# Holding back the second group's weight loads until the fifth x has been turned

## The reference

```
x = x + einsum('bct,bcd->bdt', x, L0_weights[cond])       # 32 x (128 x 128), contracts the 128 channels
x = x + einsum('bsi,boi->bso', x, L1_weight[adapter])     # 32 x (2048 x 2048), contracts the 2048 columns
```

## Time and profile before

| | |
|---|---|
| median of three executions | 1530.03 us |
| the profiled execution's own time | 1530.53 us |
| its span in the profile | 1528.7 us |
| TensorE matmul busy | 1494.1 us (98%) |
| VectorE busy | 1018.4 us (67%) |
| ScalarE busy | 512.9 us (34%) |
| GpSimd busy | 1082.0 us (71%) |
| DMA, mean over the span | 171 GB/s |
| mean granted TensorE clock | 0.992 of full |

### The profile page before, as it was taken

The page is one execution under the profiler, slowest core; times in us unless marked ns, Lnnn a source line. Parts: engine busy times, 40 slices in busy tenths (PEclk is TensorE's granted clock), DMA queues, the critical chain, the costliest instruction groups (busy, mean ns, idle before and its releaser), DMA issues.

```text
span 1528.7 us, 28816 instructions
## 1 busy us (share of the span) xinstructions
PE 1494.1 (98%) x6534; PEld 1231.5 (81%) x6535; DVE 1018.4 (67%) x637; ACT 512.9 (34%) x786; POOL 1082.0 (71%) x659
## 2 busy tenths in 40 slices
PE   5889999999999999999999999999999999999998
PEld 4668888888888888888888888888888888888887
DVE  6582879849592397794957257977768528797521
ACT  2333333333333333333333333333333333333332
POOL 4577778767685687776777578777777667787653
PEclk9979999999999999999999999999999999999999
DMA  7886899989795599897979469989788858998543
GB/s 157 171 188 145 186 188 198 182 179 191 163 206 130 130 202 181 175 202 171 200 160 205 114 153 201 189 181 204 164 186 177 168 119 177 188 204 180 126 110 86
DMA packets 287461, 261.33 MB, mean 171 GB/s; under 512 B 18648, under 2 KB 207064, under 8 KB 287448
## 3 DMA queue, kind: packets, MB, share of 16 engines
q10 hardware_dynamic: 108864, 173.06, 49.5%
q1 hardware_dynamic: 178584, 88.12, 32.6%
HBM read 227.56 MB, written 33.55 MB: 171 GB/s over the span
## 4 chain that ended last, share of the span: by engine, by line
PE 93%; SPq 2%; POOL 1%; DMA 1%; issue 1%; DVE 0%; ACT 0%; ACTq 0%; DVEq 0%
PE z_ps L686 29%; PE z_ps L687 29%; PE z_ps L695 29%; PE out_ps L707 2%; PE out_ps L704 2%; PE out_ps L705 2%; SPq L205 1%; POOL x_low L251 1%; DMA x_nat<-in_x 1%; SPq L196 0%; POOL z_low L257 0%; DMA w_nat<-in_L_cond_weight 0%; DMA ids_row<-in_itok_B 0%; SPq L213 0%; ACT z_high L333 0%
## 5 line engine op out<-in xcount | busy, mean ns | idle before, releaser
L686 PE MATMUL z_ps<-w_high,x_high 128*128 x1984 | 775.9, 391 | 8.1 <-ACT x_high L326 6.5
L687 PE MATMUL z_ps<-w_low,x_high 128*128 x1984 | 775.4, 391 | 0.0
L251 POOL TENSOR_TENSOR x_low<-x_turn,x_high 128x1024 fp32r<-128x1024 f32 x248 | 627.7, 2552 | 16.9 <-ACT x_high L326 16.6
L561 DVE STREAM_TRANSPOSE x_turn<-x_nat 128x1024 f32<-128x1024 f32 x250 | 295.7, 1220 | 454.3 <-DMA x_nat<-in_x 454.1
L695 PE MATMUL z_ps<-w_high,x_low 128*128 x1984 | 469.8, 389 | 0.0
L686 PEld LDWEIGHTS z_ps<-w_high,x_high 128*128 128x128 f32 x1984 | 374.9, 189 | 86.8 <-issue 8.8
L687 PEld LDWEIGHTS z_ps<-w_low,x_high 128*128 128x128 f32 x1984 | 374.8, 189 | 77.9
L695 PEld LDWEIGHTS z_ps<-w_high,x_low 128*128 128x128 f32 x1984 | 372.5, 188 | 77.2
L257 POOL TENSOR_TENSOR z_low<-z_raw,z_high 128x512 fp32r<-128x512 f32 x127 | 167.6, 1320 | 238.7 <-ACT z_high L333 238.7
L341 ACT ACTIVATE out_sb<-out_ps 128x512 f32<-128x512 f32 x128 | 76.5, 597 | 618.6 <-PE out_ps L707 616.6
L326 ACT ACTIVATE x_high<-x_turn 128x1024 fp32r<-128x1024 f32 x248 | 251.5, 1061 | 21.8 <-DVE x_turn L561 20.5
(11 more groups left out here) (92 smaller groups left out, 297.6 us busy)
## 6 DMA issues: line engine op xcount, KB each, us to landing
x_nat<-in_x ACTq DMA_DIRECT2D x500, 256.0 KB, 5.2
w_nat<-in_L_cond_weight SPq DMA_DIRECT2D x320, 256.0 KB, 7.7
out<-out_sb ACTq DMA_DIRECT2D x128, 256.0 KB, 5.7
a_full<-in_L_cond_weights ACTq DMA_DIRECT2D x128, 64.0 KB, 5.5
x_nat<-in_x SPq DMA_DIRECT2D x64, 64.0 KB, 3.0
ids_row<-in_itok_B SPq DMA_DIRECT2D x1, 16.0 KB, 3.0
cond_i<-in_itok_B SPq DMA_DIRECT2D x1, 0.5 KB
expert_i<-in_itok_B SPq DMA_DIRECT2D x1, 0.5 KB
```

What stands on the lines that cost most here:

```text
L251: nc.gpsimd.tensor_tensor(x_low[s][:, half], x_turn[:, half], x_high[s][:, half], ALU.subtract)\
L561: nc.vector.transpose(x_turn[:].rearrange("p (k a c) -> p k a c", a=QUAD, c=SQ)[:, blocks], x_nat[:].rearrange("p (a k c) -> p k a c", a=Q ...
L686: nc.tensor.matmul(z_ps[s][:], xs, w_high[:, ds(at + k * NC, NC)], start=(k == 0), stop=False)
L687: nc.tensor.matmul(z_ps[s][:], xs, w_low[:, ds(at + k * NC, NC)], start=False, stop=False)
```

## The change

One wait is added on SyncE, between the ramp's loads and the loop over the groups. `RAMP` is 4, and VectorE gives `x_turned` a start value of 2 * RAMP = 8, so the value 10 is reached when both halves of the fifth x have been turned.

```diff
             sp.wait_ge(tables_made, 2)
+            sp.wait_ge(x_turned, 2 * RAMP + 2)
             with sp.Fori(1, count_groups(sp)) as q:
                 row = of_group(sp, ROW, q, rows.shape[0] - NC)
                 for m in range(PIECES):
                     load_piece(q, m, row)
```

## The result

| | before | changed |
|---|---|---|
| median, 13 executions each | 1530.56 us | 1533.69 us |
| lowest to highest | 1529.52 to 1531.51 | 1532.14 to 1534.65 |
| the profiled execution's own time | 1530.53 us | 1532.14 us |
| its span | 1528.7 us | 1530.3 us |

The changed kernel is 3.1 us slower: ratio 1.002, 95% interval 1.0011 to 1.0028. The forecast was 1533.5 us, slower. The profiled execution of the changed kernel is the lowest of its thirteen, so the two profiles lie only 1.6 us apart.

What follows compares the result with a forecast made beforehand. The start of step 5 was taken as the bound: the fifth x's -4.6 us does not reach it, the new path through W and the sixth x adds 3.5, giving 1534.0 profiled, 1533.5 us median; range 1529.0 to 1536.0.

Steps and rivals of the forecast that it cites:

- The fifth x: Behind the ramp: lands at 64.4 instead of 69.0, so 4.6 us of TensorE's 6.5 us gap before step 4 go.
- SyncE's issue: After the added wait: 1.6 us of table reads, then first W issue at 68.4, fifteen us later than before.
- W's landing: First piece of W, competing with the sixth x: fourth load lands at 81.2, bounded by 75.3 and 82.5.
- third rival: Clearly slower: W's piece lands behind step 0's output too, step 5 1.3 us later still; chance 0.15.
- The piece's preparation: VectorE's work on W's first piece before turning the sixth x: 6.3 us with handovers, cast at its minimum.
- T to step 5: From T, the start of VectorE's turn of the sixth x (forecast 87.5), through GpSimd's work to step 5: 14.4 us.
- Step 5: TensorE's step 5 starts at 101.9 us instead of 98.44, 3.5 us later.
- The clock: TensorE's half clock around step 5, expected again as before: nothing in the sum, 1 us in the range.
- The time: Whole kernel: 1534.0 us for the profiled execution, 1533.5 us against the median.
- clearly slower: Piece lands behind the output and half clock reaches further into step 5: +1.3 and +1 on +3.5, 1535.6 us; chance 0.15.
- Cover: Behind step 5: W's second group, wanted by step 10, and the seventh x, turned at T + 10.6, cost nothing.
- The faster rival: W's first piece lands by about 76, decided at 76.7; step 5 4.5 us sooner, 1525.5 us; chance 0.10.

Runs made afterwards that it cites:

- the second profile: The changed kernel, unaltered, profiled and timed once more for the spread of the dates; 1533.18 us.
- shorter hold: Against the changed kernel, SyncE waits for the landing of the fifth x instead of its turn; 1528.80 us, ratio 0.999 to the kernel before.
- three x ahead: Against the changed kernel, SyncE held until the sixth x is turned too, VectorE turning sixth and seventh x before W's first piece, later ones each before a piece; 1517.92 us.
- every x ahead: Against the changed kernel, same hold, VectorE turns every x of the start ahead of the piece of W it stood behind; 1523.07 us.
- the longer hold: Against the changed kernel, SyncE waits until the low part of the fifth x is made instead of its turn; 1534.37 us, ratio 1.0023 to the kernel before.

## Why the prediction was right

- *The fifth x* was forecast to land at 64.4 and to let step 4 start at 67.0: turned from 64.11, step 4 at 66.69.
- *SyncE's issue* at 68.4: 68.12. The 1.6 us of table reads behind the wait are real, and ScalarE's first load of the sixth x, at 67.20, does come first.
- *W's landing* at 81.2: 80.5, 0.7 us less, but not for the reason given. The sum rested on loads being served about in their order of issue, with the output of step 0 behind the piece. They were not: the output, issued at 70.37, landed at 77.8, ahead of W's third load (69.16, landed 78.8) and its fourth (80.5), and so it did in the second profile.

```profile
out<-out_sb ACTq DMA_DIRECT2D x1, 256.0 KB, 7.4
```

  Nor does the stretch of the kernel before bear the rule out, once it is followed further than the earlier trace rows: from 57 to 61 us q10 moved nothing, but from 62 to 67 us the two queues moved nearly as many packets each:

```profile
q10 hardware_dynamic: 492, 0.91, 78.2%
q1 hardware_dynamic: 591, 0.29, 33.2%
```

  So the condition of the third rival, a piece that lands behind the output, came true, and its price of 1.3 us did not: nine transfers had landed 13.3 us behind the first issue, where the prediction took 13.7 for eight. That this term came out so near is in part luck.
- *The piece's preparation* of 6.3 us, with the short cast: 86.74 - 80.59 = 6.15.
- *T to step 5* of 14.4 us: 14.3, and within 0.2 in three more kernels of VectorE's old order. Its parts came as written too: A plus identity until T + 8.5, A's low part until T + 10.9, z's low part until T + 12.2.
- *Step 5* at 101.9: 101.03, 0.7 us from W's landing and the rest from the two terms above. Against 98.44 that is +2.6, not +3.5.
- *The clock* was put at nothing in the sum and 1 us in the range. Two profiles with the same step 5 differ by 1.0 us through it. In the first the step from 5 to 6 is 1.0 us shorter than in the kernel before, so only 1.6 of the 2.6 us are left in its time; in the second all are.
- *The time.* For the profiled execution the sum gave 1534.0 us; the two measured 1532.14 and 1533.18. In medians the change costs 3.1 us, 1533.69 against a forecast of 1533.5. The path was right, but that the median came within 0.2 us is luck: the step 5 of both profiles was 0.9 us before its forecast date, and 0.5 to 1.5 us of the median's loss are seen in neither profile. The mean granted clock doesn't tell the slower executions apart, it is 0.993 for 1532.14 and for 1534.38 us alike.
- *A slip of the sum*: the case called clearly slower adds up to +5.8 us, 1535.8, not 1535.6. The range holds either.
- *Cover*: the seventh x was turned at 97.36, T + 10.6 as forecast, and was not waited for; nor was W at step 10.

The faster rival fell: W landed at 80.5, where it needed 76.7. The shorter hold shows that this bound was placed well: there W landed at 76.9 and step 5 started 0.4 us before that of the kernel before.

## What to carry to other kernels

Before a transfer is held back for another's sake, look at who takes the held data, and what stands behind it in that engine's written order: here the x of step 5, long landed, waited for a W that no step before step 10 needs. A hold and a consumer's order belong together: with the order as it was the hold cost 3 us; with the sixth x taken first it gained about 4.5 us on top of the 3.5 that this order gives by itself, 8.0 together; three x ahead and a longer hold gave 12.8. Hold the part that is wanted last (here the second piece, worth 5.3 us), not the whole queue, if the order cannot be changed.

## What the runs showed of the hardware

VectorE and GpSimd took turns again at the new place: the cast of 2048 elements per partition took 1.23 us alone and 3.23 us beside `x_low`, and a GpSimd operation of 0.46 us took 2.04 us beside L611. The half clock behind TensorE's idle stretch of 11.5 to 12.5 us ended at different points in two profiles of the same kernel: granted clock 0.69 or 0.80 in the same 10 us at the same work, 1.0 us of time. A transfer of 256 KB issued later on one queue could land ahead of an earlier one on the other: the output by 1.0 us, though issued 1.2 us behind W's third load. And SyncE's issues of DMAs were slower at one place of the changed kernel: the fourth load of W was issued 2.9 us behind the first, against 1.6 before. It is not enough for that that both queues have work, for at 113.78 us of the kernel before and with every x ahead four loads were issued within 1.6 us beside four of x. It cost the landing little: with every x ahead W's fourth load, issued in 1.6 us, landed at 80.1.

What stays open: which dates make ten of the change's thirteen executions slower than both its profiles; why the longer hold, 3 us later in T in both its profiles, lies only 0.7 us above the change in the median of its eight executions; and what slowed SyncE's issues.
